# Other turns for the weight loads, v of the first quads straight from SBUF, and dummy matmuls in the first stage

## The reference

```
x = x + layernorm(attn(layernorm(x)))
x = x + layernorm(ffn(layernorm(x)))
attn: q, k, v = x @ (alpha * sign(W)).T + b
      y = softmax(q k^T / 4) v;  y @ (alpha * sign(Wp)).T + bp
ffn:  h = silu(x w1^T s1) * (x w2^T s2)
      h = gelu(h h1^T s);  h = gelu(h h2^T s);  h w3^T s3
```

## Time and profile before

| | us |
|---|---|
| median of three runs (lowest, highest) | 1269.09 (1268.47, 1270.46) |
| the profiled execution | 1268.14 |
| its span | 1266.3 |
| PE busy in the span | 1202.3 (95%) |
| DVE busy | 637.0 (50%) |
| ACT busy | 726.7 (57%) |
| mean granted clock of PE, as a share | 0.974 |

### The profile page before, as it was taken

The page is one execution under the profiler, slowest core; times in us unless marked ns, Lnnn a source line. Parts: engine busy times, 40 slices in busy tenths (PEclk is TensorE's granted clock), DMA queues, the critical chain, the costliest instruction groups (busy, mean ns, idle before and its releaser), DMA issues.

```text
span 1266.3 us, 17763 instructions
## 1 busy us (share of the span) xinstructions
PE 1202.3 (95%) x6705; PEld 738.5 (58%) x6705; DVE 637.0 (50%) x1211; ACT 726.7 (57%) x871; POOL 46.5 (4%) x53
## 2 busy tenths in 40 slices
PE   6597999799979997999999999999999999999998
PEld 4132333233323321325888888888888888888886
DVE  7253534353434302533556747656566476565624
ACT  6696999699969997896224234243242342432421
POOL 6001000101010000000000000000000000000000
PEclk9698999899989998998999999999999999999999
DMA  5975868785786777611000101001001011010000
GB/s 187 228 182 185 198 108 191 185 194 97 189 199 122 166 134 155 123 49 59 23 12 29 39 2 34 34 1 48 19 21 47 1 34 34 1 34 1 17 1 18
DMA packets 53339, 107.57 MB, mean 85 GB/s; under 512 B 6790, under 2 KB 23558, under 8 KB 53238
## 3 DMA queue, kind: packets, MB, share of 16 engines
q1 hardware_dynamic: 52956, 105.93, 35.1%
q10 hardware_dynamic: 288, 0.39, 0.1%
HBM read 71.90 MB, written 45.88 MB: 93 GB/s over the span
## 4 chain that ended last, share of the span: by engine, by line
PE 53%; DVE 1%; issue 0%; ACT 0%; POOLq 0%; DVEq 0%
PE ffn_ps L1659 24%; PE ffn_ps L1658 23%; PE ffn_ps L1687 2%; PE ffn_ps L1686 2%; PE side_ps L1642 1%; PE side_ps L1651 0%; DVE ln_stats L1887 0%; DVE zn L1898 0%; DVE zn L1895 0%; DVE zn L1885 0%; PE ffn_ps L1700 0%; PE ffn_ps L1701 0%; DVE ln_mean_var L1889 0%; ACT hid L1772 0%; DVE h_lo L1912 0%
## 5 line engine op out<-in xcount | busy, mean ns | idle before, releaser
L1241 ACT ACTIVATE probs<-s_ps 128x1024 f32<-128x1024 f32 x512 | 476.0, 1115 | 66.1 <-PE s_ps L1088 65.3
L1659 PE MATMUL ffn_ps<-h_lo,W 128*128 128x512 f32 x1024 | 405.9, 396 | 0.0
L1658 PE MATMUL ffn_ps<-h_hi,W 128*128 128x512 f32 x1024 | 403.0, 394 | 0.0
L1100 PE MATMUL y_ps<-probs,v_st 128*17 128x512 f32 x2048 | 278.4, 617 | 29.9 <-DVE y_sb L1266 29.0
L1659 PEld LDWEIGHTS ffn_ps<-h_lo,W 128*128 128x128 f32 x1024 | 192.0, 188 | 47.5
L1088 PE MATMUL s_ps<-q_st,k_st 50*128 50x512 f32 x1024 | 207.5, 472 | 12.8 <-DMA v_st<-v_scr 12.3
L1772 ACT ACTIVATE hid<-ffn_ps,scales 128x512 f32<-128x512 f32 x128 | 81.1, 686 | 240.0 <-PE ffn_ps L1659 235.0
L1658 PEld LDWEIGHTS ffn_ps<-h_hi,W 128*128 128x128 f32 x1024 | 191.9, 187 | 45.7
L1088 PEld LDWEIGHTS s_ps<-q_st,k_st 50*128 50x128 f32 x1024 | 88.5, 189 | 216.8 <-ACT probs L1241 171.2
L1918 DVE CAST h_hi<-hid 128x512 fp32r<-128x512 f32 x128 | 53.5, 418 | 192.8 <-ACT hid L1772 192.6
L1912 DVE TENSOR_TENSOR h_lo<-hid,h_hi 128x512 fp32r<-128x512 f32 x192 | 130.1, 684 | 1.1
(11 more groups left out here) (173 smaller groups left out, 892.8 us busy)
## 6 DMA issues: line engine op xcount, KB each, us to landing
k_st<-qk_scr SPq DMA_DIRECT2D x90, 128.0 KB, 6.4
q_st<-qk_scr SPq DMA_DIRECT2D x90, 128.0 KB, 7.0
w_scr<-ffn_w SPq DMA_DIRECT2D x16, 704.0 KB, 9.0
W<-w_scr SPq DMA_DIRECT2D x16, 704.0 KB, 6.2
y_scr<-y_sb SPq DMA_DIRECT2D x32, 256.0 KB, 2.2
qk_scr<-y SPq DMA_DIRECT2D x24, 256.0 KB, 7.3
qk_scr<-sums SPq DMA_DIRECT2D x24, 256.0 KB, 8.7
v_st<-v_scr SPq DMA_DIRECT2D x16, 272.0 KB, 9.8
```

The source lines that it names most:

```text
L1100: i = pe.matmul(y_ps[32 * j:32 * j + VCOLS, :], v_st[g % 2][:, s, VCOLS * j:VCOLS * (j + 1)], probs[(PAIRS * turn + j // 2) % PROBS][:, j ...
L1241: act.activation(probs[a % PROBS][:, :, :], s_ps[a % 3][:, :, :], ACT.Exp, scale=SCALE)\
L1658: pe.matmul(bank_of(t)[:, :], w, hi[:, k, :].bitcast(form), start=(k == 0), stop=False)
L1659: mm = pe.matmul(bank_of(t)[:, :], w, lo[:, k, :].bitcast(form), start=False, stop=last)
```

## The change

Four things are changed.

The turns of the weight loads and of their checks are others: loads at 9, 25, 30 and 41 instead of 5, 18, 30 and 42, checks at 15, 35, 39 and 50 instead of 12, 24, 36 and 51. Batch 0 gets a new place row for its first block, and for its second block the row of the other batches.

In the first stage SP copies quad 0's v from `v_aug` to `v_st` within SBUF, instead of storing all of `v_aug`; the two stores to `v_scr` now stand in the attention part behind `load_xb(0)`, where the load of `v_st` stood. `pv` of turn 0 waits for the two copies (`v_loaded`), the load of quad 1 for the stores.

PE gets 49 matmuls of the identity with itself into a part of `qk_ps` that nobody reads then: 20 ahead of the first transposition, 4 and 7 around the transposition of `top`, 18 behind the matmul of `bound` at the end of the stage. The first 4 wait for `qk_copied`, since they write to `qk_ps`.

The semaphore of `group_top` and that of `square` become one, with doubled counts.

```diff
--- before.py
+++ after.py
@@ -55,11 +55,12 @@
 
 
 EARLY, LATE = -4, -2
-FIRST_BLOCK = (Places(0, 3, (7, 9), (12, 14, 17, 20), (23, 25), 28), Places(EARLY, LATE, (1, 3), (6, 9, 13, 17), (20, 22), 25))
-SECOND_BLOCK = (Places(27, 29, (31, 33), (35, 38, 41, 44), (47, 49), 52), Places(24, 26, (28, 30), (33, 37, 41, 44), (47, 49), 52))
+FIRST_BLOCK = (Places(0, 2, (4, 6), (9, 12, 15, 17), (20, 22), 25), Places(EARLY, LATE, (1, 3), (6, 9, 13, 17), (20, 22), 25))
+SECOND_BLOCK = Places(24, 26, (28, 30), (33, 37, 41, 44), (47, 49), 52)
 AT_TOP, AT_SPREAD = 54, 57
-AT_W = (5, 18, 30, 42)
-AT_CHECK = (51, 12, 24, 36)
+KEEP_GOING = (20, 4, 7, 18)
+AT_W = (9, 25, 30, 41)
+AT_CHECK = (15, 35, 39, 50)
 EPS = 1e-5
 SCALE = HEAD_DIM ** -0.5
 
@@ -139,6 +140,7 @@
     part: object
     v_aug: object
     v_stored: object
+    v_loaded: object
 
 
 def x_by_block(x):
@@ -205,7 +207,7 @@
 
 STACK_LOADS = 2 * 2 * PARTS
 QUAD_LOADS = STACK_LOADS + 1
-FIRST_EXTRA = STACK_LOADS
+FIRST_EXTRA = STACK_LOADS - 1
 
 
 def m_loads_of(g):
@@ -268,6 +270,7 @@
                 v_aug=[until_w.enter_context(nc.sbuf_tensor(f"v_aug{u}", [P, HEADS // QUAD, TILES, QUAD, VCOLS], F32))
                        for u in range(BATCH_BLOCKS)],
                 v_stored=keep.enter_context(nc.semaphore("first_v_stored")),
+                v_loaded=keep.enter_context(nc.semaphore("first_v_loaded")),
             )
             project(nc, x, attn_w, attn_wT, attn_b, attn_b_rows, ffn_s, ffn_s3, c, qk_scr, v_scr, m_scr, quads, first)
         W = sb("W", [P, W_ALL], F32R)
@@ -413,10 +416,10 @@
                 sp.dma_start(qk_rows[s, 0, c, :, :, u * BLK:(u + 1) * BLK],
                              part[s][u][:, 2 * c:2 * c + 2, :].bitcast(F32)).then_inc(done, 16)
 
-            def store_v(u):
+            def load_first_v(u):
                 sp.wait_ge(aug_done, u + 1)
-                sp.dma_start(v_rows[0, :, :, TILES * u:TILES * (u + 1), :].rearrange("q p s n -> p q (s n)"),
-                             v_aug[u][:, :, :, :, :].rearrange("p q t j n -> p q (t j n)")).then_inc(v_stored, 16)
+                sp.dma_start(quads.v[0][:, TILES * u:TILES * (u + 1), :],
+                             v_aug[u][:, 0, :, :, :].rearrange("p t j n -> p t (j n)")).then_inc(first.v_loaded, 16)
 
             for u in range(BATCH_BLOCKS):
                 sp.dma_start(x_in[u][:, :, :], x_blk[u]).then_inc(x_loaded[u], 16)
@@ -448,12 +451,12 @@
             sp.wait_ge(lo_first_stored, 16)
             load_rows(sp, 0, LO, 0)
             load_rows(sp, 1, LO, 0)
-            store_v(0)
+            load_first_v(0)
             sp.wait_ge(hi_stored, 16 * BATCH_BLOCKS)
             load_rows(sp, 0, HI, 1)
             sp.wait_ge(lo_stored, 16)
             load_rows(sp, 0, LO, 1)
-            store_v(1)
+            load_first_v(1)
             sp.wait_ge(shift_done, 1)
             for hh in range(2):
                 at = hh * HALF + STACK
@@ -711,7 +714,13 @@
                                   start=(s == 0), stop=(s == QK - 1))
                 i.then_inc(norms_done, 1)
 
+            def keep_going(n):
+
+                for _ in range(n):
+                    pe.matmul(qk_ps[:, 0, 0:P], ident[:, :], ident[:, :], start=True, stop=True)
+
             pe.wait_ge(ident_set, 1)
+            keep_going(KEEP_GOING[0])
             turn_x(0)
             mean_weights()
             project_qk(0, 0)
@@ -724,10 +733,14 @@
             pe.wait_ge(filled, 4)
             sum_squares(0)
             sum_squares(1)
+            pe.wait_ge(qk_copied, QK * BATCH_BLOCKS)
+            keep_going(KEEP_GOING[1])
             pe.wait_ge(top_done, 1)
             pe.transpose(top_ps, top[:, :], ident[0:2 * HEADS, 0:2 * HEADS]).then_inc(top_turned, 1)
+            keep_going(KEEP_GOING[2])
             pe.wait_ge(root_done, 1)
             pe.matmul(bound_ps, ones[:, :], bound[:, :], start=True, stop=True).then_inc(bound_spread, 1)
+            keep_going(KEEP_GOING[3])
 
 
 def attention(nc, const, qk_scr, v_scr, m_scr, y_scr, ffn_w, w_scr, W, quads, first, x, tail_in):
@@ -819,7 +832,6 @@
         hi_done = sem("pj_hi_done")
         lo_done = sem("pj_lo_done")
         square_done = sem("pj_square_done")
-        group_done = sem("pj_group_done")
         part_stored = [sem(f"part_stored{i}") for i in range(2)]
         v_done = sem("pj_v_done")
         v_read = sem("pj_v_read")
@@ -860,7 +872,7 @@
         def blocks_of(b):
 
             late = min(b - 1, 1)
-            return ((0, BATCH_BLOCKS * (b - 1), FIRST_BLOCK[late]), (1, BATCH_BLOCKS * (b - 1) + 1, SECOND_BLOCK[late]))
+            return ((0, BATCH_BLOCKS * (b - 1), FIRST_BLOCK[late]), (1, BATCH_BLOCKS * (b - 1) + 1, SECOND_BLOCK))
 
         @block.sync
         def _(sp):
@@ -876,6 +888,7 @@
                 g = b * QUADS_OF_BATCH
                 if b == 0:
                     sp.wait_ge(stored, 16 * REST_STORES)
+                    sp.wait_ge(first.v_stored, 16 * (BATCH_BLOCKS + 1))
                 sp.wait_ge(loaded[0], loads_of(g))
                 sp.wait_ge(m_loaded[0], m_loads_of(g))
                 sp.wait_ge(shift_stored, 16 * (b + 1))
@@ -975,8 +988,9 @@
                     sp.dma_start(tail_in.x1[:, :, :], x_blk[0]).then_inc(tail_in.x_loaded[0], 16)
 
             load_xb(0)
-            sp.wait_ge(first.v_stored, 16 * (BATCH_BLOCKS + 1))
-            load_v(sp, v_scr, quads, 0, 0)
+            for u in range(BATCH_BLOCKS):
+                sp.dma_start(v_rows[0, :, :, TILES * u:TILES * (u + 1), :].rearrange("q p s n -> p q (s n)"),
+                             first.v_aug[u][:, :, :, :, :].rearrange("p q t j n -> p q (t j n)")).then_inc(first.v_stored, 16)
             sp.dma_start(m_scr[0, 0:HEADS], shift[:, :].bitcast(F32)).then_inc(shift_stored, 16)
             for s in range(2):
                 for u in range(BATCH_BLOCKS):
@@ -1094,6 +1109,8 @@
                 n, s = divmod(turn, ST)
                 g = n // BATCH_BLOCKS
                 pe.wait_ge(probs_ready, PAIRS * (turn + 1))
+                if turn == 0:
+                    pe.wait_ge(first.v_loaded, 16 * BATCH_BLOCKS)
                 if s == 0 and n:
                     pe.wait_ge(y_copied, n)
                 for j in range(QUAD):
@@ -1141,7 +1158,7 @@
 
             def sum_squares(n):
                 pe.wait_ge(v_read, CT * (n + 1))
-                pe.wait_ge(square_done, QK * (n + 1))
+                pe.wait_ge(square_done, 2 * QK * (n + 1))
                 for m in range(QK):
                     i = pe.matmul(norm_ps, const.gather[:, m, :], square[:, m, :], start=(m == 0), stop=(m == QK - 1))
                 i.then_inc(norms_done, 1)
@@ -1312,10 +1329,10 @@
                 dve.tensor_tensor(part_lo[:, slot, :], qk[slot][:, :], part_hi[:, slot, :], ALU.subtract)\
                     .then_inc(lo_done, 1)
                 if k > 1:
-                    dve.wait_ge(square_done, k - 1)
+                    dve.wait_ge(square_done, 2 * (k - 1))
                 dve.tensor_reduce(group_top[:, :], qk[slot][:, :].rearrange("p (a b) -> p a b", b=GROUP), AX.X,
-                                  ALU.max, apply_absolute_value=True).then_inc(group_done, 1)
-                dve.wait_ge(group_done, k)
+                                  ALU.max, apply_absolute_value=True).then_inc(square_done, 1)
+                dve.wait_ge(square_done, 2 * k - 1)
                 if m == 0 and n:
                     dve.wait_ge(norms_done, n)
                 dve.tensor_tensor(square[:, m, :], group_top[:, :], group_top[:, :], ALU.mult)\
@@ -1457,12 +1474,8 @@
                         projected(b + 1, t)
                     else:
                         prepared(t)
-                    if t in AT_CHECK[1:]:
-                        i = len(AT_W) * b + AT_CHECK.index(t) - 1
-                        check_w(2 * i)
-                        check_w(2 * i + 1)
-                    if t == AT_CHECK[0]:
-                        i = len(AT_W) * b + len(AT_W) - 1
+                    if t in AT_CHECK:
+                        i = len(AT_W) * b + AT_CHECK.index(t)
                         check_w(2 * i)
                         check_w(2 * i + 1)
             copy_y(HALVES - 1)
```

## The result

The changed kernel takes 1233.99 us (median of four runs, 1232.79 to 1238.68), the kernel before 1268.78 beside it: a ratio of 0.9732, 95% interval 0.9703 to 0.9760. The forecast was 1234, its range 1226 to 1243. The profiled execution took 1232.98, its span is 1231.1 against 1266.3.

The account below looks back on a forecast made before the run. Late weight loads held VectorE's in-order checks and so the copy TensorE needs, before about 580 us. 26.6 + 6.5 - 1.0 - 2.5 + 5.0 + 0.7 = 35.3 us off 1268.14 gave 1232.8, as median 1234, range 1226 to 1243.

Parts of the forecast that it names:

- 26.6 minus 2.5 forecast: Batches 0 to 2: stalls at copy 25 go, gaining 26.6 us; a new stall in batch 0 costs 2.5.
- The first cost: Batch 0, copy 17: third split, check and copy in a row make the copy 1.7 us late.
- second cost: Batch 0: the third split waits for the first part's store; both costs together 0 to 5 us, charged 2.5.
- 2.3 of stall stays, 1.8 of slow clock, and 0.8: Last batch, copy 17: remaining stall, slow clock behind it and later landing, 4.9 us kept of an 11.4 loss.
- the 1.0: Last batch, copy 41: two checks ahead make it 1.8 us late, partly hidden by ScalarE; charged 1.0.
- 5.7 forecast: Start: first scores 5.0 us sooner, at about 39.6, plus 0.7 for the clock.
- the 0.7 for the clock: First scores to turn 5: the clock can give 0 to 2.3 us; 0.7 taken.
- second `x_lo` 1.4 us sooner: Start: the 20 first dummies speed the first projections, bringing the second x_lo 1.4 us sooner, between 0 and 1.9.
- the dummies don't do what they are for: Rival, start: dummies don't lift the clock or delay x; 1.4 + 0.7 us go, 1236, inside the forecast.
- a change of the FFN's 686 us: Sign of a wrong forecast: the FFN, which the change doesn't touch, takes other than 686 us.
- new stalls in batches 1 and 2: Rival, turns 15 and 39: late load or part store costs 4 to 5 us per place; 1238 to 1246, chance 0.20.
- the late load everywhere: Rival: load of turn 9 lands so late that copy 17 stalls in all four batches; 1270 or more, chance 0.02.

Follow-up runs that it names:

- e9: The kernel before with only the change's new turns of weight loads and checks (old places, old v, no dummies): 1235.69 us, ratio 0.9744.
- the best version: The change with checks at 19, 35, 42 and 50, the last batch's FFN loads at turn 12, and 8 matmuls ahead of the FFN: 1222.11 us.
- e6: The change with the last batch's loads of y and a block of x for the FFN issued at turn 12 instead of 1: 1228.36 us.
- e12: The change once more, unchanged, on one chip beside the best version: 1233.65 us.
- e2: The change without any of the 49 dummy matmuls: 1233.62 us.
- e1: The change with loads back at turns 5, 18, 30, 42 and checks at 12, 24, 36, 51: 1267.81 us, ratio 0.9986 to the kernel before.
- e10: The change with checks at 19, 35, 42 and 50 and 8 matmuls ahead of the FFN, without the 49 first-stage dummies: 1222.85 us.
- e5: The change with quad 0's v on its old way, stored to scratch and loaded behind the barrier: 1239.47 us.

## Why the prediction was right, and where its steps weren't

*Batches 0 to 2.* 26.6 minus 2.5 forecast, so 24.1; measured 7.3 + 9.0 + 8.7 = 25.0. In batch 0 the turns alone gave 8.8 (e9) against 9.0. The sum could leave out how waits, checks and slow clock overlap, because the window from copy to copy has all three in it.

*The new stall of batch 0.* 2.5 forecast, in two costs. From copy 9 to 49 the change takes 82.13; the best version, with the same places and the check behind the copy, takes 80.33: 1.8. The first cost, split and check and copy in a row, was the main one. PE's wait at copy 17 was 1.71 us here, 2.03 in e6, 2.14 in e12 and 2.42 in e2, and the split's wait for the store of the part 0.28, 0.61, 0.71 and 0.99: without that second cost 1.4 is left in each, where I had worked out 1.7. In e1 the second cost was 3.78, so the upper bound of 5 had a reason.

*The last batch.* The mechanism held (e6), two sizes didn't. The step "2.3 of stall stays, 1.8 of slow clock, and 0.8" makes 4.9; it was 4.2 + 1.8 = 6.0. The stall of 2.3 was the smallest that this place shows: the same order of instructions gave 17.01 in the kernel before and 19.59 in e1, and the load at turn 9 gave 18.8 to 19.2 in five other traces. I had read one execution as if its landing were a constant. And copy 41 cost 2.3 instead of 1.0. PE's wait was 1.5 us in all seven traces with the check at 39, near the 1.8 worked out. What the 1.0 left out is the clock behind it. Where it stayed at 1.00 (e6, e9), the next eight turns took 14.2 us instead of 14.7, and the whole cost 1.0 as charged; in the change it fell to 0.89 and they took 15.4. Gain 3.2 instead of 5.5: the largest error.

*The start.* 5.7 forecast, 5.8 measured, by other terms. The first scores came 6.4 us sooner, not 5.0; but one execution differs from the next by 1.4 there (e12), so the 1.4 too much is no more than that. The kernel before varies too: e9 has its first stage unchanged, and its first scores came 1.0 sooner than in the trace of the kernel before:

```profile
43.79 1.65 PE L1088 MATMUL s_ps<-q_st,k_st 50*128 50x512 f32 x6 [12.34 <-DMA v_st<-v_scr]
```

What is late next was named as `shift`; of the ten traces with direct v and nothing else ahead of the scores it was the memset of `y_ps` behind the barrier in four and `shift` in six, within the same 38.4 to 39.9 us. From the first scores to the first copy it took 20.2 against 19.5 before, so the 0.7 for the clock isn't seen; the same kernel took 19.5 in e12, so 0.7 lies within what one trace differs from another. The 1.4 for the dummies stood in the sum as "second `x_lo` 1.4 us sooner". It was (17.55 against 18.94), yet without any dummies it also comes at 18.38 (e2), 17.78 (e10) and 17.80 (e9): the term was read from one late execution. With dummies it lies at 17.55 to 17.64 in all ten traces, so they bring 0.1 to 1.4 there. The rival *the dummies don't do what they are for*, priced at 2.1, was right about their worth. Direct v is worth the 5 us: 5.5 to 5.8 by the medians of e5, 3.9 to 5.4 at the first scores.

*Behind the last copy* I counted nothing, and 1.3 came: the slow clock at the start of the FFN was shorter (0.86 in the first 12 us instead of 0.72). The prediction read the 19th slice of the earlier trace rows as part of the attention and the FFN as undisturbed. But that slice runs from 569.8 to 601.5 us, and its low clock lies behind the barrier at 582.7, in the FFN's first microseconds, as this window of the kernel before shows:

```profile
582.70:591.00 8.30, 8.29 (x24) 6.58 (x25) 2.10 (x3) 3.75 (x5) 0.00 (x0) 0.63 0.51 143
```

So this term was put at nothing by a misreading. The prediction had named a change of the FFN's 686 us as a sign of being wrong. It came, though the FFN's program is the same: the length of the slow clock there varies between executions (683.3 to 686.3 in all traces without dummies ahead of it). It made up by chance for half of the last batch's error. Measured less forecast, the terms are +0.9 for batches 0 to 2, -2.3 for the last, +0.1 for the start and +1.3 here, which cancel. That the total agrees to 0.1 us is luck; the terms agree to about 2, and the interval of the ratio alone is 7 us wide.

*The rivals of new stalls in batches 1 and 2, and of the late load everywhere,* didn't come true: the intervals up to copies 17 and 41 of batches 1 and 2 lie within 0.1 us of the kernel before in all seven traces with the checks at 15 and 39.

The parts don't add up to the whole: the turns alone bring 34 us by the medians, the change 35 (36 beside them on the same chip), although undoing direct v alone costs 5.5. By the traces of e9 and the change, 6.8 at the start are reduced by 1.6 from the places of batch 0, 1.3 from the clock behind copy 41 and 1.6 from the clock at the FFN; the last two are the chance of single executions. The new places with the checks at 19, 35 and 42 cost nothing. Whether the old places would be better still in the best version wasn't tried.

## What to carry to other kernels

When an engine works in order and looks at a transfer only to verify it, the look belongs behind the work that another engine waits for, not ahead of it: two numbers (15 to 19, 39 to 42) brought 9 us. A late landing is cured in the queue, by what is issued ahead of it. Dummy matmuls paid here, by the traces, where TensorE bounds the stage behind the gap and they could shorten the gap; ahead of a stage that is held by transfers or ScalarE nothing of them was seen. And a stall or a landing read from one execution is no constant: ask how far it spreads before it becomes a term of a sum.

## What the runs showed of the hardware

- The same DMA of 704 KB lands 5.1 us (e6) or 14.0 us (the change) after its issue, by what stands ahead of it, and 17.1 or 18.5 with the same instructions ahead of it (before, e1).
- A gap of 2.65 to 2.75 us of TensorE ahead of the FFN was followed by a low granted clock in nine of eleven traces and not in the other two, with the same instructions next to it. 2.05 us of dummies in the gap, which left 1.1 us idle, kept it in three of three.
- A stall of 1.50 us at copy 41 of the last batch was followed, over 15.5 us, by a mean clock of 0.89 in four traces, 0.78 in one and 1.00 in two, and the next eight turns took 15.4 to 15.6, 16.8 and 14.2 us.
- From the first scores to the first copy, where ScalarE is busy for 17.7 to 17.9 us, it took 19.5 to 20.4 us in twelve traces with a mean clock of 0.76 to 0.88, and 22.2 and 21.6 at 0.71 and 0.70 (e5, e9). Among the twelve the clock doesn't order the times: 20.2 and 19.5 both have 0.83 (the change, e12).
